# A mixture-of-experts layer on one core: the input stream issued first, 17 key levels for 23, one folded chunk of weights more, and another order of two products

## The reference, cut to what matters

```
x_rot  = hamilton(q_left_n, hamilton(fft-filter(x), q_right_conj))    # a 4x4 rotation per quarter of D, with one gate
probs  = softmax(x_rot @ gate_w.T)
R      = probs - rank for the experts of a token whose mass ahead is under 0.9, else -1e9
keep   = the 512 tokens with the largest R, for each expert
h      = gelu(x_rot @ w1[e].T)
y      = sum over e of  (probs if assigned and kept else 0) * (h @ w2[e].T)
out    = x + y
```

## Time and profile before

| | |
|---|---|
| median of 3 runs | 267.33 us (266.39 to 267.89) |
| profiled execution | 266.72 us, of which the trace spans 264.9 us |
| TensorE's mean granted clock | 0.993 of full speed |
| TensorE matmul busy | 243.7 us (92%) |
| VectorE busy | 199.4 us (75%) |
| ScalarE busy | 149.8 us (57%) |
| GpSimd busy | 137.0 us (52%) |
| chain that ended last | TensorE 68%, VectorE 16%, DMA 8%, issue 2% |

### The profile page before, as it was taken

The page is one execution under the profiler, slowest core; times in us unless marked ns, Lnnn a source line. Parts: engine busy times, 40 slices in busy tenths (PEclk is TensorE's granted clock), DMA queues, the critical chain, the costliest instruction groups (busy, mean ns, idle before and its releaser), DMA issues.

```text
span 264.9 us, 4043 instructions
## 1 busy us (share of the span) xinstructions
PE 243.7 (92%) x1450; PEld 185.0 (70%) x1450; DVE 199.4 (75%) x430; ACT 149.8 (57%) x275; POOL 137.0 (52%) x105
## 2 busy tenths in 40 slices
PE   7788878798998999999999999999999999999970
PEld 2455433245996888888888888888888888888750
DVE  5288889998989967978996798789779966933220
ACT  6431048864566658746765774687467658734100
POOL 1000000037703987887778749766875771487530
PEclk9999999999999999999999999999999999999997
DMA  6999999407798597579658855973994690372521
GB/s 214 422 424 428 503 343 387 149 21 196 261 317 282 195 344 132 161 179 273 166 82 249 241 111 118 294 192 48 219 249 130 85 222 12 42 85 37 182 91 40
DMA packets 12787, 53.81 MB, mean 203 GB/s; under 512 B 2768, under 2 KB 3152, under 8 KB 9552
## 3 DMA queue, kind: packets, MB, share of 16 engines
q1 hardware_dynamic: 4512, 35.72, 37.2%
q0 software_dynamic: 8256, 17.85, 31.8%
HBM read 44.78 MB, written 18.22 MB: 238 GB/s over the span
## 4 chain that ended last, share of the span: by engine, by line
PE 68%; DVE 16%; DMA 8%; issue 2%; POOL 1%; ACT 1%; SPq 0%; POOLq 0%; DVEq 0%
PE bank L828 21%; PE bank L830 20%; PE bank L829 20%; DMA region<-in_xt 7%; DVE region L691 4%; PE bank L810 4%; DVE w1rot L509 3%; DMA xg<-in_x,gath 1%; PE bank L888 1%; POOL xg L298 1%; DVE hl L538 1%; DVE thr L708 1%; DVE xg L637 0%; DVE xg L633 0%; DVE csum L638 0%
## 5 line engine op out<-in xcount | busy, mean ns | idle before, releaser
L314 POOL DMA_INDIRECT out<-ysb,scat x32 | 61.3, 1916 | 34.8 <-ACT ysb L391 22.2
L509 DVE SCALAR_TENSOR_TENSOR w1rot<-w1raw,rot,w1rot 128x512 f32<-128x512 f32 x84 | 63.1, 751 | 5.3 <-ACT w1rot L351 3.4
L298 POOL DMA_INDIRECT xg<-in_x,gath x16 | 19.8, 1235 | 70.5 <-DVE gath L560 56.3
L828 PE MATMUL bank<-xh,w1h 128*128 128x512 f32 (+1 forms) x144 | 53.2, 370 | 0.1
L830 PE MATMUL bank<-xh,w1l 128*128 128x512 f32 (+1 forms) x144 | 52.7, 366 | 0.0
L829 PE MATMUL bank<-xl,w1h 128*128 128x512 f32 (+1 forms) x144 | 52.7, 366 | 0.0
L828 PE MATMUL bank<-w2h,hh 128*128 128x512 f32 x128 | 51.6, 403 | 0.0
L830 PE MATMUL bank<-w2h,hl 128*128 128x512 f32 x128 | 50.0, 390 | 0.0
L829 PE MATMUL bank<-w2l,hh 128*128 128x512 f32 x128 | 49.9, 390 | 0.0
L538 DVE TENSOR_TENSOR hl<-hf,hh 128x512 fp32r<-128x512 f32 x32 | 22.1, 689 | 28.3 <-ACT hh L382 28.3
L378 ACT ACTIVATE hf<-bank 128x512 f32<-128x512 f32 x32 | 19.1, 597 | 36.1 <-PE bank L830 36.1
(11 more groups left out here) (134 smaller groups left out, 332.7 us busy)
## 6 DMA issues: line engine op xcount, KB each, us to landing
region<-in_xt SPq DMA_DIRECT2D x8, 1024.0 KB, 9.4
w1raw<-in_w SPq DMA_DIRECT2D x8, 1024.0 KB, 12.0
w2raw<-in_w SPq DMA_DIRECT2D x8, 1024.0 KB, 8.6
score<-probs_scratch,pidx POOLq DMA_INDIRECT x32, 5.1
out<-ysb,scat POOLq DMA_INDIRECT x32, 6.0
probs_scratch<-probs SPq DMA_DIRECT2D x1, 384.0 KB, 21.1
ch<-in_ch SPq DMA_DIRECT2D x1, 320.5 KB, 10.2
xg<-in_x,gath POOLq DMA_INDIRECT x16, 4.0
```

The source lines that it names most:

```text
L298: pool.indirect_dma_start(xg[e % 2][:, s, :], None, x_d, bass.IndirectOffsetOnAxis(gath[:, e, s:s + 1], 0)).then_inc(xg_in[e % 2][s], 16)
L314: pool.indirect_dma_start(out_d, bass.IndirectOffsetOnAxis(scat[:, e, s:s + 1], 0), ysb[:, s, :], None, compute_op=ALU.add if e < LAST els ...
L509: ins = nc.vector.scalar_tensor_tensor(dst, w1raw[:, e % 2, i, :], rot[:, j, i:i + 1], dst, ALU.mult, ALU.add)
L828: nc.tensor.matmul(dst, ah, bh, start=first, stop=False)
```

## The change

1. **Start.** `small` and `cf` are issued by ScalarE's program; SP's first DMA is `load_x(0)`. TensorE's first filler is 12 products, not 13.
2. **Levels.** The bins are fewer: TL = 17, so L654 compares 1088 elements and the counts have 136 columns. Bins from 1.25 up are twice as wide; the search therefore multiplies by a factor `scale` that depends on `top`: one operation more before `keys`, two more in round 0.
3. **Slots.** `count_tokens(0, 2)` reads the thresholds from PSUM (`kbank`) and the copy to `tb` follows it. `gath` is written from `tabg` directly, without the limit to N - 1 (x in DRAM gets 128 rows of zeros behind it), and the rest of `slot_tables` follows.
4. **Fold.** Chunk 0 of expert 1's w1 is folded on TensorE by four folds that stand where the 9 and the 8 filler products stood, into bank 2; ScalarE's `w1_folded(0, 1)` copies it ahead of `x_high0(0)`. ScalarE's `w1_first(1, 0)` and VectorE's `rotate_w1(1, 0)` are gone. The remaining fillers write other banks, and `layer1_half(0)`, which writes bank 2, also waits for that copy.
5. **Layer 1.** A block first makes the products with the high part of x (4 chunks, w1h and w1l), then those with the low part. The first block waits for `x_hi` first and for `x_lo` only before the low part's products.
6. **Layer 2 of expert 0.** `layer2(0, 1)` stands ahead of the transposes of expert 1's chunks 2 and 3.

The core of the diff:

```diff
-KEY_ULP = 2.0 ** -24
+KEY_ULP = 2.0 ** -23
...
-WIDTH = 0.125
+WIDTH, WIDTH1 = 0.25, 0.125
...
-            sp.dma_start(small[:, :], small_d).then_inc(small_in, 16)
...
-            sp.dma_start(cf[:, :], cf_d).then_inc(cf_in, 16)
...
         def _(act):
+            act.dma_start(small[:, :], small_d).then_inc(small_in, 16)
+            act.dma_start(cf[:, :], cf_d).then_inc(cf_in, 16)
...
-                if j == 0:
+                if j == 0 or e == 1:
                     act.wait_ge(w1_in[e % 2], 16 * (e // 2 + 1))
                     act.wait_ge(w1_lo, C4 * e)
...
-            def w1_folded(j):
-
-                act.wait_ge(fold_mm, j + 1)
-                nc.scalar.activation(w1rot[:, j, :], fbank[j][:, :], ACT.Copy).then_inc(w1_rot, 1)
+            def w1_folded(j, e=0):
+
+                act.wait_ge(fold_mm, C4 * e + j + 1)
+                act.wait_ge(w1_lo, C4 * e)
+                nc.scalar.activation(w1rot[:, j, :], fbank[C4 * e + j][:, :], ACT.Copy).then_inc(w1_rot, 1)
...
             nc.scalar.activation(warm[:, :], cfv("ident")[:, 0:1], ACT.Gelu)
+            w1_folded(0, 1)
             x_high0(0)
             x_high0(1)
             rows_out(1, 2, E)
             x_high0(2)
-            w1_first(1, 0)
...
+                nc.vector.tensor_tensor(gath[:, e, :], tabg[:, :], vbank[:, :, NT], ALU.add).then_inc(gath_ready, 1)
                 then(nc.vector.tensor_tensor(tabf[:, :], tabg[:, :], vbank[:, :, NT], ALU.add))
-                nc.vector.tensor_scalar(gath[:, e, :], tabf[:, :], float(N - 1), None, ALU.min).then_inc(gath_ready, 1)
...
             dve.wait_ge(key_mm, 1)
-            nc.vector.tensor_scalar(keys[:, :], kbank[:, 0:N // TC], top[:, 0:1], -1.0, ALU.subtract,
+            then(nc.vector.tensor_scalar(scale[:, 0:1], top[:, :], SPLIT, -2.0, ALU.is_ge, ALU.add))
+            nc.vector.tensor_scalar(keys[:, :], kbank[:, 0:N // TC], top[:, 0:1], scale[:, 0:1], ALU.subtract,
                                     ALU.mult).then_inc(thr_ready, 1)
...
-                if r >= 1:
+                if r == 0:
+
+                    nc.vector.tensor_scalar(scale[:, 1:2], scale[:, 0:1], 3.0, -0.5, ALU.add, ALU.mult)
+                    nc.vector.tensor_scalar(scale[:, 2:3], scale[:, 0:1], 3.0, -0.5 * KEY_ULP, ALU.add, ALU.mult)
+                else:
...
-            then(nc.vector.tensor_copy(tb[:, :], kbank[:, 0:E]))
             dve.wait_ge(ch_in, 16)
-            count_tokens(0, 2)
+            count_tokens(0, 2, kbank)
+            nc.vector.tensor_copy(tb[:, :], kbank[:, 0:E])
...
                     slot_tables(2)
-                    rotate_w1(1, 0)
...
                 for j in range(C4):
-                    if f == 0 and e >= 1:
+                    if f == 0:
+                        pe.wait_ge(x_hi, C4 * e + j + 1)
+                    nc.tensor.matmul(dst, w1h[e % 2][:, j, fs], xh[:, j, :], start=(j == 0), stop=False)
+                    nc.tensor.matmul(dst, w1l[e % 2][:, j, fs], xh[:, j, :], start=False, stop=False)
+                for j in range(C4):
+                    if f == 0:
                         pe.wait_ge(x_lo, C4 * e + j + 1)
-                    last = split_product(hbank[n % 2][:, :], w1h[e % 2][:, j, fs], w1l[e % 2][:, j, fs],
-                                         xh[:, j, :], xl[:, j, :], j == 0, j == C4 - 1)
+                    last = nc.tensor.matmul(dst, w1h[e % 2][:, j, fs], xl[:, j, :], start=False, stop=(j == C4 - 1))
...
                 if n == 0:
                     pe.wait_ge(w1_lo, C4)
-                    pe.wait_ge(x_lo, S4 // 2)
-                if n == 2:
-                    pe.wait_ge(x_lo, S4)
+                    pe.wait_ge(w1_rot, C4 + 1)
+                if n % 2 == 0:
+                    pe.wait_ge(x_hi, S4 // 2 * (1 + n // 2))
...
-            keep_clock(2, cbank[1])
+            keep_clock(2, cbank[0])
             slot_rows(0)
-            keep_clock(9, cbank[1])
+            pe.wait_ge(w1_in[1], 16)
+            fold(0, 0, 1)
+            fold(0, 1, 1)
             slot_rows(1)
-            keep_clock(8, cbank[1])
+            fold(0, 2, 1)
+            fold(0, 3, 1)
             transpose_x0(0)
-            keep_clock(3, cbank[1])
+            keep_clock(3, obank)
...
                 layer2(e, 0)
+                if e == 0:
+                    layer2(e, 1)
                 if e + 1 < E:
                     transpose_x(e + 1, (2, 3))
-                for s in range(1, S4):
+                for s in range(2 if e == 0 else 1, S4):
                     layer2(e, s)
```

More of the change, by code:

```diff
@@ L85 @@
 CG, NCG = table(("sel", E), ("slot", S4), ("start", KT), ("need", KT), ("step", ROUNDS * KT), ("offset", ROUNDS * KT),
-                ("last", 1), ("tops", NL))
+                ("tops", NL))
 CA, NCA = table(("same", P), ("ones", P), ("levels", NL))
@@ L201, in build @@
         pbank, lbank, rbank, nbank = bank[1:3], [bank[0], bank[3]], bank[4:6], bank[7]
-        fbank, kbank, cbank, obank, dbank = [bank[i] for i in (0, 3, 4, 5)], bank[6], bank[1:3], bank[3], bank[7]
+        fbank, kbank, cbank, obank, dbank = [bank[i] for i in (0, 3, 4, 5, 2)], bank[6], bank[1:3], bank[3], bank[7]
         HALF = CAP // 2
@@ L701, in _ @@
                 else:
-                    nc.vector.tensor_scalar(edge[:, 0:1], base[:, now, 0:1], -1.0, top[:, 0:1], ALU.mult, ALU.add)
+                    nc.vector.tensor_scalar(edge[:, 0:1], base[:, now, 0:1], scale[:, 1:2], top[:, 0:1], ALU.mult, ALU.add)
                 dve.wait_ge(cnt_mm, r + 1)
@@ L711, in _ @@
                 else:
-                    nc.vector.scalar_tensor_tensor(edge[:, 1:2], cgv("last"), best[:, :], edge[:, 0:1],
+                    nc.vector.scalar_tensor_tensor(edge[:, 1:2], scale[:, 2:3], best[:, :], edge[:, 0:1],
                                                    ALU.mult, ALU.add).then_inc(base_ready, 1)
@@ L858, in layer1_half @@
                     fs = slice(f * P, (f + 1) * P)
+                    dst = hbank[n % 2][:, i * HALF:(i + 1) * HALF]
                     for j in range(C4):
-                        last = split_product(hbank[n % 2][:, i * HALF:(i + 1) * HALF], w1h[0][:, j, fs], w1l[0][:, j, fs],
-                                             xh[:, j, ns], xl[:, j, ns], j == 0, j == C4 - 1)
+                        nc.tensor.matmul(dst, w1h[0][:, j, fs], xh[:, j, ns], start=(j == 0), stop=False)
+                        nc.tensor.matmul(dst, w1l[0][:, j, fs], xh[:, j, ns], start=False, stop=False)
+                    if n % 2 == 0 and i == 0:
+                        pe.wait_ge(x_lo, S4 // 2 * (1 + n // 2))
+                    for j in range(C4):
+                        last = nc.tensor.matmul(dst, w1h[0][:, j, fs], xl[:, j, ns], start=False, stop=(j == C4 - 1))
                 last.then_inc(h_mm, 1)
@@ L914, in count_levels, with fold @@
                 last.then_inc(lev_mm, 1)
-            def fold(j, i):
-                term = nc.tensor.matmul(fbank[j][:, :], diag[:, j * C4 + i, :], w1raw[:, 0, i, :],
+            def fold(j, i, e=0):
+                term = nc.tensor.matmul(fbank[C4 * e + j][:, :], diag[:, j * C4 + i, :], w1raw[:, e, i, :],
                                         start=(i == 0), stop=(i == C4 - 1))
@@ L1046, in shape_constants @@
     sign = np.where(act, -1.0, 1.0)
-    tops = np.array([o + WIDTH for _, o in BINS])
-    cg[:, slice(*CG["start"])] = -tops[0] * sign
+    lead = WIDTH1 - G9
+    tops = np.array([o + WIDTH1 - lead if at < SPLIT else o + WIDTH - 2 * lead for at, o in BINS])
+    cg[:, slice(*CG["start"])] = -2 * lead * sign
     cg[:, slice(*CG["need"])] = np.where(act, 2.0 * CAP - N, CAP)
@@ L1076 @@
     from concourse.bass_utils import run_bass_kernel_spmd
-    rows = np.ascontiguousarray(np.asarray(x).reshape(N, D))
-    xt = np.ascontiguousarray(rows.reshape(P, NG, TPG, C4, P).transpose(1, 4, 3, 2, 0)).reshape(NG, P, C4, TG)
+    rows = np.concatenate([np.asarray(x).reshape(N, D), np.zeros((P, D), np.float32)])
+    xt = np.ascontiguousarray(rows[0:N].reshape(P, NG, TPG, C4, P).transpose(1, 4, 3, 2, 0)).reshape(NG, P, C4, TG)
     cond, right = np.asarray(cond_256).T, np.asarray(L0_cond_q_right).T
```

20 lines of the change are left out of this document (9 added, 11 removed).

## The result

| | before | after |
|---|---|---|
| median of the runs | 267.3 us (266.39 to 267.89) | 271.56 us (270.17 to 272.54, 4 runs) |
| ratio to before | | 1.0158, 95% interval 1.0098 to 1.0219 |
| profiled execution | 266.72 us, span 264.9 | 272.32 us, span 270.5 |
| mean granted clock | 0.993 | 0.979 |

A forecast was written before the change was run, and what follows sets the result against it. TensorE is full from expert 1 on, so gains lie in the chain of waits ahead of 85 us; 0.61 + 0.41 + 0.38 + 1.23 = 2.63 us off the 267.33 median gives 264.7 us, range 263.4 to 265.9.

The forecast's parts named there:

- Start: Input loads: x issued 0.89 us sooner, less 0.28 for sharing with the small loads; 0.61 us gained, between 0 and 0.89.
- Rival B: Start gives nothing because `cf` and `small` come 1 us later beside x; 265.3 us, or 266.1 at its low end; chance 0.17.
- ends before the gate's wait: TensorE's start: the shorter first filler costs nothing, as it ends before the first gate's wait.
- Rival D: Clock falls to 1.2 GHz between the slot rows if folds count for less than fillers; 267.7 us, chance 0.04.
- Levels: Search on VectorE: smaller comparisons and counts, less one added operation before `keys`; 0.41 us gained, between 0.2 and 0.6.
- Slots: Slot tables: mask no longer waits for the `tb` copy, `gath` starts a step sooner; 0.38 us gained, 0.2 to 0.4.
- Layer 1: Expert 0: the first product no longer waits for the low part of group 1; 0.30 us sooner.
- Layer 2 of expert 0: `layer2(0, 2)` starts at 84.20, not 85.43, limited by the scores; 1.23 us together with layer 1, ends 0.8 and 1.73.
- the scores move with the gathers: Layer 2 of expert 0: the gathered scores `y_out(0, 0)` waits for until 83.50 follow the gathers, not TensorE.
- Folds: TensorE between slot rows: folds keep it as busy as fillers, pace and clock unchanged; 0 us.
- Rivals A and C: A: scores don't hold TensorE, start gains all issue time, 263.9, chance 0.14; C: scores land behind weights, 269.7, 0.03.
- gate 5 near 20.2 and `keys` near 34.2: Signs of the forecast: TensorE's gate for x group 5 near 20.2 us, and `keys` starting near 34.2 us.

The follow-up runs named there:

- the kernel of the split issue: Changed kernel with `small` issued by SP ahead of x and `cf` by ScalarE; 264.81 us, ratio 0.9931; run again later, 267.10 us, ratio 0.9736.
- part 1 taken back: Changed kernel with `small` and `cf` issued by SP ahead of x again, 12 fillers kept; 266.28 us, ratio 0.993.
- part 1 alone: Kernel before with only part 1 added: `small` and `cf` issued by ScalarE, x first on SP, 13 fillers; 273.17 us, ratio 1.0241.
- both behind x: Changed kernel with `small` and `cf` issued by SP behind x group 0 and ahead of the second group; 268.79 us, ratio 1.008.
- no fold: The kernel of the split issue with part 4 undone, fillers in place of expert 1's folds; 264.83 us, ratio 0.9928.
- the first eight experiments: The experiments from part 1 taken back to that with SP's bulk copies waiting for expert 0's scores, each beside the kernel before; 264.32 to 273.17 us.
- weights first: The kernel of the split issue, bulk copies waiting for expert 0's scores, expert 1's `w2` and expert 2's `w1` issued ahead; 269.47 us, later 267.71.

## Why the prediction was wrong

**Start: the step that failed.** It read: the two loads "now share the way with x: 0.121 MB at 425 GB/s is 0.28 us". It priced bytes on the way of x, and never when the small loads would themselves land. They landed 5.5 and 7.9 us after their issue, 1.8 and 2.1 us before. That put `gfold` 5.75 us back, with TensorE idle for 5.38 us ahead of the first gate. Chunk 2 began 6.08 us later instead of 0.61 sooner, outside both ends of the term (0 and 0.89), and taking part 1 back gave 5.3 us by the medians. *Rival B* had the mechanism, at a chance of 0.17, and a mistake of the same kind in its size: "1 us later", and no loss against the kernel before. Counted in packets, as an estimate, it would have been 9 x 0.31 = 2.8 us for each of the two loads, one behind the other: 5.6 for `cf`, which was 5.8 us later than alone, and 2.8 for `small`, which was 3.7 us later.

**The clock.** The first filler "ends before the gate's wait" held only while `gfold` was early. This is a cover whose loss was not priced: 2.34 us in the profiles, 2.7 by the medians. Rival D looked for a fall of the clock at another place, between the slot rows, where there was none.

**Levels** (0.41): 0.43. L652 took 0.72 us for 1088 elements, as 0.70 was foretold. **Slots** (0.38): 0.28; the term was 0.1 too large. **Layer 1** (0.30): 0.37.

**Layer 2 of expert 0** (0.93 of the 1.23): +0.45 in the changed kernel. The step "the scores move with the gathers" was right to within 1.3 us only: from the first gather to `y_out` were 26.30 us before and 27.57 after. In the changed kernel the eighth gather of x took 2.83 us where its neighbours take 0.95, so SP's bulk copies, and the scores behind them, were later: the copies were issued 14.54 us behind the first gather, 12.93 before. In the kernel of the split issue it took 0.95 and the stretch was 20.24, 0.76 shorter than before: the term is mis-sized by 0.17 there, on one profile. That the longer gather is the cause is only argued, from five profiles that have it (the changed kernel, part 1 taken back, part 1 alone, both behind x, no fold): all five took 26.85 us or more from the first product of layer 1 in expert 0 to that in expert 1, and the four others of the first eight experiments 25.01 to 25.81. The last profile of weights first has the longer gather too and took 25.00; there the bulk copies stand behind the scores. What the prediction did not see is that its two means, order and fold, remove one wait between them.

**Folds** (0): right for TensorE; four folds took 1.96 and 1.96 us, with no fall of the clock. **Rivals A and C** did not come. The tests named in the prediction, gate 5 near 20.2 and `keys` near 34.2, were nearly met by the kernel of the split issue (20.34 and 34.35), in which x starts 0.46 us earlier and the small loads are not behind it.

## What to carry to other kernels

A small load that starts a chain belongs ahead of the large ones in the DMA engines' work, on whichever queue; price a load by its own landing time among the packets beside it, not by its bytes. A second engine may issue a load at the same moment as the first small one (`cf` here), at no loss that could be measured and no gain either, but it should not be used to let the large load pass. And an engine's filler must cover the worst case of the wait, or its clock is lost with the time.

## What was not expected of the hardware

One GpSimd gather instruction was held in every profile, and ended 12.0 to 12.4 us behind the start of the first gather. It was either the eighth gather of x (2.82 to 2.84 us instead of 0.95) or the first gather of scores (1.89), in the same kernel now one, now the other: in the kernel of weights first the score gather in one profile, the x gather in the next. What holds it is open.

A load on a queue of its own landed later than on the queue of the large loads: `cf` 7.9 us after its issue by ScalarE, 4.4 by SP behind 1 MB of x.
